# One region of rows moved to a multiple of 128 bytes, and two linear maps of the vector part joined into one, in a four-layer graph network

## The reference

```python
s_in = jnp.concatenate([agg[..., 0], agg[..., 1]], axis=1)
v_in = jnp.concatenate([agg[..., 2:5], agg[..., 5:8]], axis=1)
os1 = s_in @ w_f2o1_s / math.sqrt(2 * F)
ov1 = jnp.einsum('nmc,mb->nbc', v_in, w_f2o1_v) / math.sqrt(2 * F)
os1 = ssp(os1)                                   # softplus(x) - log 2
os2 = os1 @ w_f2o2_s / math.sqrt(B)
ov2 = jnp.einsum('nbc,bd->ndc', ov1, w_f2o2_v) / math.sqrt(B)
return jnp.concatenate([os2, ov2.reshape(n, -1)], axis=-1)
```

## Time and profile before

| | us |
|---|---|
| median of 3 runs | 2288.8 (2287.68 to 2291.94) |
| profiled execution | 2287.86 |
| its span, first to last instruction | 2285.8 |

### The profile page before, as it was taken

One profiled execution on the slowest core, in us unless ns is written; L12 is line 12 of the kernel. 1 busy time (PEld: TensorE's weight loads), 2 busy tenths in 40 slices (PEclk: granted clock), 3 DMA queues, 4 the chain that ended last, 5 costly groups with the idle time before them and its releaser, 6 DMA issues.

```text
span 2285.8 us, 36469 instructions
## 1 busy us (share of the span) xinstructions
PE 2223.5 (97%) x12307; PEld 1892.1 (83%) x12307; DVE 1487.8 (65%) x4613; ACT 1023.7 (45%) x2044; POOL 943.0 (41%) x931
## 2 busy tenths in 40 slices
PE   7999999979999999999999999999999999999996
PEld 6878778858899888888999999988887777778785
DVE  7777777754766856665345665267776776667675
ACT  3982112222365632222225665334444665666454
POOL 2017637745223234366532222023545554552542
PEclk9999999989999999999999999999999999999998
DMA  6434575443477758786226665456667776666541
GB/s 210 139 137 135 143 200 189 156 139 101 145 237 240 259 170 275 266 270 221 86 78 210 234 236 211 134 187 228 208 211 235 249 257 225 211 231 210 167 124 65
DMA packets 192415, 435.82 MB, mean 191 GB/s; under 512 B 45607, under 2 KB 74542, under 8 KB 191694
## 3 DMA queue, kind: packets, MB, share of 16 engines
q1 hardware_dynamic: 126954, 249.08, 31.9%
q0 software_dynamic: 65296, 184.67, 25.9%
HBM read 242.68 MB, written 190.96 MB: 190 GB/s over the span
## 4 chain that ended last, share of the span: by engine, by line
PE 67%; DVE 5%; ACT 3%; issue 2%; DMA 1%; POOL 0%; DVEq 0%; ACTq 0%; SPq 0%; POOLq 0%
PE g_h_ps L2575 7%; PE g_h_ps L2592 7%; PE g_h_ps L2577 6%; PE g_h_ps L2576 6%; PE g_h_ps L2593 6%; PE g_h_ps L2594 6%; PE g_h_ps L2617 5%; PE g_h_ps L2619 5%; PE g_h_ps L2618 5%; PE g_t_ps L77 4%; PE g_h_ps L1748 2%; PE g_h_ps L1750 2%; PE g_h_ps L1749 2%; PE g_sum_ps L995 1%; PE g_sum_ps L996 1%
## 5 line engine op out<-in xcount | busy, mean ns | idle before, releaser
L2709 ACT ACTIVATE g_act_t<-g_t_ps,g_b_col 128x256 f32<-128x256 f32 (+1 forms) x488 | 201.9, 466 | 398.3 <-PE g_t_ps L77 398.0
L2592 PE MATMUL g_h_ps<-g_x_hi,held_w_hi 128*128 128x256 f32 x1216 | 352.1, 290 | 0.0
L2593 PE MATMUL g_h_ps<-g_x_lo,held_w_hi 128*128 128x256 f32 x1216 | 343.8, 283 | 0.0
L2594 PE MATMUL g_h_ps<-g_x_hi,held_w_lo 128*128 128x256 f32 x1216 | 343.8, 283 | 0.0
L607 DVE CUSTOM_DVE_ANT_0 g_prod<-g_h_sb,g_a_rows 128x256 f32<-128x256 f32 x632 | 224.1, 419 | 78.4 <-ACT g_h_sb L498 70.8
L2617 PE MATMUL g_h_ps<-fc_w_hi,g_x_hi 128*128 128x512 f32 x632 | 270.9, 429 | 3.0 <-DVE fc_z L2995 2.2
L2575 PE MATMUL g_h_ps<-held_w_hi,g_x_hi 128*128 128x512 f32 x656 | 263.5, 402 | 0.0
L2577 PE MATMUL g_h_ps<-held_w_hi,g_x_lo 128*128 128x512 f32 x656 | 256.7, 391 | 0.0
L2576 PE MATMUL g_h_ps<-held_w_lo,g_x_hi 128*128 128x512 f32 x656 | 256.5, 391 | 0.0
L429 PE MATMUL g_h_ps<-g_w_hi,g_x_hi 128*128 128x512 f32 x616 | 243.4, 395 | 8.9 <-DVE g_x_lo L593 7.3
L2619 PE MATMUL g_h_ps<-fc_w_hi,g_x_lo 128*128 128x512 f32 x632 | 249.9, 395 | 0.0
(11 more groups left out here) (400 smaller groups left out, 4864.1 us busy)
## 6 DMA issues: line engine op xcount, KB each, us to landing
h<-g_h_sb SPq DMA_DIRECT2D x120, 512.0 KB, 4.5
g_x_in<-in_dram SPq DMA_DIRECT2D x40, 512.0 KB, 3.9
h<-g_rows_own SPq DMA_DIRECT2D x40, 512.0 KB, 5.0
h_cols<-g_h_sb SPq DMA_DIRECT2D x38, 512.0 KB, 5.3
xb_rows<-in_dram SPq DMA_DIRECT2D x19, 1024.0 KB
xb<-xb_rows SPq DMA_DIRECT2D x19, 1024.0 KB, 4.4
g_x_in<-h_cols SPq DMA_DIRECT2D x38, 512.0 KB, 6.7
g_x_in<-h SPq DMA_DIRECT2D x21, 512.0 KB, 5.8
```

What stands on the lines that cost most here:

```text
L2592: pe.matmul(out, wh, xh, start=(k == 0), stop=False)
L2593: pe.matmul(out, wh, xl, start=False, stop=False)
L2594: last = pe.matmul(out, wl, xh, start=False, stop=(k == KC - 1))
```

## The change

It has two parts. The first is in the layout: `Space.align` is new, and `node_layers` calls it with 128 before it takes `rows_at`, which then is 169344 = 1323 x 128. Everything from there to the end of the space moves up by 64 bytes.

The second is in painn. As no nonlinearity stands between the two maps of the vector part, their weights are multiplied on chip once: `join_weights` makes the 64x128 product in PSUM, and DVE scales it into `ov`. `w_f2o1_v` is loaded turned (`o1v_t`, 128x64) for that. `out_one` keeps the scalar part alone; `copy_sums_t` writes the turned vector sums into one of four buffers `vecs_t`, of 64 partitions, and `out_two` multiplies these by `ov`. The buffers `hid` and the copy into them go.

```diff
+        sb.align(P)
         rows_at = sb.end
...
     def out_one(self, pe, t):
...
-            pe.wait_ge(self.w_scaled, 2)
+            pe.wait_ge(self.w_scaled, 3)
...
-        pe.matmul(h.o1_ps[:, 0:P], h.o1s[:, :], h.sums_t[:, 0, :], start=True, stop=True)
-        pe.matmul(h.o1_ps[:, P:4 * P], h.o1v[:, :], h.sums_t[0:2 * f, 1:4, :], start=True, stop=True).then_inc(self.o1_done, 1)
+        pe.matmul(h.o1_ps[:, 0:P], h.o1s[:, :], h.sums_t[:, :], start=True, stop=True).then_inc(self.o1_done, 1)
+
+    def join_weights(self, pe):
+
+        h, f = self.hold, self.F
+        pe.wait_ge(self.w_in, 16 * 8)
+        pe.matmul(h.o1_ps[0:2 * f, 0:P], h.o1v_t[:, :], h.o2v[:, :], start=True, stop=True).then_inc(self.o1_done, 1)
...
         for c in range(3):
-            pe.matmul(h.o2_ps[:, (1 + c) * b:(2 + c) * b], h.hid[t % 4][:, c, :], h.o2v[:, :], start=True, stop=True)
+            pe.matmul(h.o2_ps[:, (1 + c) * b:(2 + c) * b], h.vecs_t[t % 4][:, c, :], h.ov[:, :], start=True, stop=True)
...
     def copy_sums_t(self, act, t):
...
+        if t >= 4:
+
+            act.wait_ge(self.o2_done, t - 3)
...
     def copy_hidden(self, act, t):
...
-            act.wait_ge(self.o2_done, t - 3)
             act.wait_ge(self.scal_done, t // 2 - 1)
-        act.activation(h.hid_s[t // 2 % 2][:, t % 2, :], h.o1_ps[:, 0:P], ACT.Copy)
-        act.activation(h.hid[t % 4][:, :, :].rearrange("p c e -> p (c e)"), h.o1_ps[:, P:4 * P], ACT.Copy).then_inc(self.o1_out, 1)
+        act.activation(h.hid_s[t // 2 % 2][:, t % 2, :], h.o1_ps[:, 0:P], ACT.Copy).then_inc(self.o1_out, 1)
...
-        dve.tensor_scalar(h.o1v[:, :], h.o1v_raw[:, :], (2 * f) ** -0.5, None, ALU.mult).then_inc(self.w_scaled, 1)
+        dve.wait_ge(self.o1_done, self.JOINED)
+        dve.tensor_scalar(h.ov[:, :], h.o1_ps[0:2 * f, 0:P], (2 * f) ** -0.5, None, ALU.mult).then_inc(self.w_scaled, 1)
...
+                    if g == PAINN_W + 3 * KC:
+                        pe.wait_ge(signals.finished, e2.past(ET, ET))
+                        painn.join_weights(pe)
+                    if g == CONV:
+                        pe.wait_ge(painn.w_scaled, 3)
```

More of the change, by code:

```diff
@@ L72, in __call__, with align @@
         return tensor
+    def align(self, unit):
+        self.end = -(-self.end // unit) * unit
 def turn_whole(pe, out, rows, ident):
@@ L1338 @@
     AHEAD = 4
+    JOINED = 1
     B = P
@@ L1389, in load_weights @@
             sp.dma_start(h.o1s_raw[(1 + c) * f:(2 + c) * f, :], self.w_o1s[f:2 * f, :]).then_inc(self.w_in, 16)
-        sp.dma_start(h.o1v_raw[:, :], self.w_o1v).then_inc(self.w_in, 16)
+        sp.dma_start(h.o1v_t[:, :], self.w_o1v).then_inc(self.w_in, 16)
         sp.dma_start(h.o2s[:, :], self.w_o2s).then_inc(self.w_in, 16)
@@ L1481, in out_one @@
     def out_one(self, pe, t):
-        h, f = self.hold, self.F
+        h = self.hold
         if t == 0:
-            pe.wait_ge(self.w_scaled, 2)
+            pe.wait_ge(self.w_scaled, 3)
         pe.wait_ge(self.st_out, 2 * t + 2)
@@ L1488, in out_one @@
             pe.wait_ge(self.o1_out, t)
-        pe.matmul(h.o1_ps[:, 0:P], h.o1s[:, :], h.sums_t[:, 0, :], start=True, stop=True)
-        pe.matmul(h.o1_ps[:, P:4 * P], h.o1v[:, :], h.sums_t[0:2 * f, 1:4, :], start=True, stop=True).then_inc(self.o1_done, 1)
+        pe.matmul(h.o1_ps[:, 0:P], h.o1s[:, :], h.sums_t[:, :], start=True, stop=True).then_inc(self.o1_done, 1)
[3 more added lines that the diff above has]
+        pe.matmul(h.o1_ps[0:2 * f, 0:P], h.o1v_t[:, :], h.o2v[:, :], start=True, stop=True).then_inc(self.o1_done, 1)
     def out_two(self, pe, t):
-        h, b = self.hold, self.B
+        h, b, f = self.hold, self.B, self.F
         pe.wait_ge(self.o1_out, t + 1)
@@ L1539, in copy_sums_t @@
         if t:
-            act.wait_ge(self.o1_done, t)
-        act.activation(h.sums_t[:, 0, :], h.turn_ps[:, 0:P], ACT.Copy).then_inc(self.st_out, 1)
-        act.activation(h.sums_t[0:2 * f, 1:4, :].rearrange("p c e -> p (c e)"), h.turn_ps[0:2 * f, P:4 * P],
+            act.wait_ge(self.o1_done, self.JOINED + t)
+        if t >= 4:
+            act.wait_ge(self.o2_done, t - 3)
+        act.activation(h.sums_t[:, :], h.turn_ps[:, 0:P], ACT.Copy).then_inc(self.st_out, 1)
+        act.activation(h.vecs_t[t % 4][:, :, :].rearrange("p c e -> p (c e)"), h.turn_ps[0:2 * f, P:4 * P],
                        ACT.Copy).then_inc(self.st_out, 1)
@@ L1547, in copy_hidden @@
         h = self.hold
-        act.wait_ge(self.o1_done, t + 1)
+        act.wait_ge(self.o1_done, self.JOINED + t + 1)
         if t >= 4:
-            act.wait_ge(self.o2_done, t - 3)
             act.wait_ge(self.scal_done, t // 2 - 1)
-        act.activation(h.hid_s[t // 2 % 2][:, t % 2, :], h.o1_ps[:, 0:P], ACT.Copy)
-        act.activation(h.hid[t % 4][:, :, :].rearrange("p c e -> p (c e)"), h.o1_ps[:, P:4 * P], ACT.Copy).then_inc(self.o1_out, 1)
+        act.activation(h.hid_s[t // 2 % 2][:, t % 2, :], h.o1_ps[:, 0:P], ACT.Copy).then_inc(self.o1_out, 1)
     def softplus(self, act, i):
@@ L2097, in node_layers @@
         p.u = split_rows(big("u", [P, 4 * 8 * F]), 4, 8 * F)
-        p.hid = [big(f"hid{s}", [P, 3, P]) for s in range(4)]
-        p.x_t, p.sums_t = big("x_t", [P, 4, P]), big("sums_t", [P, 4, P])
+        p.vecs_t = [big(f"vecs_t{s}", [2 * F, 3, P]) for s in range(4)]
+        p.x_t, p.sums_t = big("x_t", [P, 4, P]), big("sums_t", [P, P])
         p.pmsg = big("msg", [P, 10 * F])
@@ L2111, in node_layers @@
         low = Space(nc, "painn", small_at)
-        p.o1s, p.o1v, p.o2s, p.o2v = (low(n, [rows, P]) for n, rows in (("o1s", P), ("o1v", 2 * F), ("o2s", P), ("o2v", P)))
-        p.o1s_raw, p.o1v_raw = low("o1s_raw", [P, P]), low("o1v_raw", [2 * F, P])
+        p.o1s, p.ov, p.o2s, p.o2v = (low(n, [rows, P]) for n, rows in (("o1s", P), ("ov", 2 * F), ("o2s", P), ("o2v", P)))
+        p.o1s_raw, p.o1v_t = low("o1s_raw", [P, P]), low("o1v_t", [P, 2 * F])
         p.w_in_sb = low("w_in", [P, 2, F])
@@ L3224 @@
            g(0, "Wfc"), g(0, "bfc"), g(1, "weight"), np.stack([g(2, "w_in2f_s"), g(2, "w_in2f_v")], 1),
-           g(2, "W1"), g(2, "b1")[:, None], pw2, g(2, "w_f2o1_s"), g(2, "w_f2o1_v"), g(2, "w_f2o2_s"),
+           g(2, "W1"), g(2, "b1")[:, None], pw2, g(2, "w_f2o1_s"), g(2, "w_f2o1_v").T, g(2, "w_f2o2_s"),
            g(2, "w_f2o2_v"), g(3, "W").T, g(3, "b")]
```

## The result

| | us |
|---|---|
| before, median of 4 runs | 2290.37 (2287.68 to 2292.65) |
| changed kernel, median of 4 runs | 2270.14 (2268.23 to 2273.96) |
| ratio | 0.9923, 95% interval 0.9909 to 0.9937 |

By the ratio the change saves 17.6 us (14.4 to 20.8). The two medians lie 20.2 us apart, at the upper end of that interval; the profiled executions, which the rest of this text takes apart, took 2287.86 and 2270.06 us, 17.8 apart. The forecast was 22.5: right in direction, and the time lies in the range of 2260 to 2275, but the gain is 5 us smaller than forecast. The rest of this text finds these 5 us.

What follows compares the result with a forecast made beforehand. PE bounds the kernel, except in the conv stretch, where it already waits. Alignment 9.8 + edge sums 0.5 + joined map 12.0 - join 0.3 + shorter waits 0.5 = 22.5 us saved: 2266 us, own range 2262 to 2270, wider range 2260 to 2275.

Steps and rivals of the forecast that it cites:

- What bounds the kernel: fc, conv and painn stretches: PE bounds, so time off PE is time off the end, except in conv, where PE waits.
- rival 2: Painn stretch: DVE or ACT becomes the bound, PE waits for half of what it saved; 16.5 us gained, 2272; chance 0.11.
- The joined map: Painn tiles: removing L1490 saves 0.98 us, 64-row ends in out_two cost 0.38; net 0.60 a tile, 12.0 for 20.
- Rival 3: Painn tiles: the 0.33 us at L1490's ends was its own, not following the 64 rows; 7.6 us more, 2258; chance 0.07.
- 1896 x 5.7 ns = 10.8 us: fc products: with streamed weights on a multiple of 128 bytes, each of 1896 matmuls saves 5.7 ns.
- "half" of the conv stretch: fc with conv: alignment worth 2.1 us over 372 matmuls, half counted because PE idles 6 us; 10.8 - 1.0 = 9.8.
- given 0.5 back: Painn: PE's 2.0 us of waits for ACT's copy of the sums shrink by 0.5 us (bounds nothing and 2.0).
- The join there: fc tile 23: one matmul of two passes, 0.22 us, with one wait; 0.3 us of cost counted for everything.
- The edge sums' 0.5 us: Edge sums of the two earlier layers: 80 matmuls streaming src_hi gain 6 ns each from alignment, 0.5 us.
- Rival 1: fc products: the address does not make 233 of 227 ns; 12.2 us are left, 2276; chance 0.07.
- Rival 5: Painn stretch: PE idles between tiles, granted clock falls to 1.2 GHz, kernel slower, up to 2410; chance 0.02.

Runs made afterwards that it cites:

- 128-row version: Changed kernel with painn's vector part on 128 rows: two whole transposes, out_two's vector part as two matmuls against a block-diagonal joined map; 2265.53 us, ratio 0.9904.
- last version: 128-row version with x 64 bytes further on only in macro tiles whose products stream x over the held weights; 2255.31 us, ratio 0.9857.
- rows 32k: Changed kernel with x and the region 32 bytes higher, row k of fc_hi and fc_lo 32k bytes past the place alike to x; 2281.05 us, one run.
- faster version: Changed kernel with painn's vector work on whole 128-row passes instead of 64-row ones; 2265.53 us, ratio 0.9904.

## Why the prediction was right, and where it was wrong

**What bounds the kernel** was read rightly for two of three stretches. In the fc stretch and, less what PE's waits for the sums grew by, in the painn stretch time taken off PE reached the end. That the total still lies in the range is partly luck: the forecast's own range ended at 2270, and what lies above it was put in for rival 2, not for an alignment of half the size.

**The joined map** came out as worked: 0.98 - 0.38 = 0.60 us a tile was forecast, 12.3 us / 20 = 0.61 measured on PE's lines, and both numbers of the chain (0.86 and 0.42) are the ones named beforehand. That the ends of the 64-row work move with it is shown by the passes beside it and by taking the 64-row work away. The Trainium skill's "TensorEngine Tiling (Array Packing)", section "Key Properties", said that a change of mode drains the array, and the trace agrees: the passes at the two ends stand at 202 to 213 ns where those in the middle stand at 112, and of the 0.46 us a tile by which the 128-row version's lines are shorter, 0.36 are these ends (the rest is the transpose that it saves). That a drain is what fills them no run shows. Rival 3 is out.

**The step that failed** is the alignment's "1896 x 5.7 ns = 10.8 us", less "half" of the conv stretch. Alone it measures 4.6 us (2.7 to 6.6) where 9.8 + 0.5 stood. Three things were off, by the changed kernel's trace:

- The conv stretch. I saw PE idle for 6 us there and took half of its 2.1 us. It gave nothing: from step 412 to step 468 the changed kernel is 4.2 to 4.6 us ahead throughout, so a chain through ACT and DVE sets the pace there, and PE waits for `conv_t_lo`. The run at another pace shows it: six fc steps to a conv step take these waits away. The other kernels, at five steps, show it too: where the clock held, the stretch took 175.6 us in each of them, whether the fc products stood at 233 ns (before, the joined map alone), at 232 (rows 16 bytes apart, the region at 256) or at 228 (the last version). That is 0.0 in place of +1.0. With the fall of the clock it is -1.1: the stretch took 176.7 to 177.2 us in each of the five kernels where the clock fell once in it, and 178.4 where it fell twice.
- The painn stretch. fc products stood at 230 ns in the mean there, not 228, and its 396 products gave 1.1 us in place of 2.3. PE's waits for the sums rose by 1.0 us, where I had given 0.5 back, and that took the 1.1 away again. This rise belongs to the joined map: these waits are 3.0 us with the joined map alone too, 2.2 with the alignment alone and 2.0 before. What holds the distance at 230 ns in this stretch wasn't tried.
- The size: from one fc product to the next 5.3 ns in the fc stretch rather than 5.7 (233.4 to 228.1 in the mean), and nothing where transposes stand between two of them, beside some 150 of the 1032: 4.9 us in place of 5.9. The join there costs 0.36 where 0.3 was counted.

The edge sums' 0.5 us didn't come: 392 and 394 ns, where 396 and 392 stood before. Both their operands lie in the region and moved together, so by what the runs showed nothing changed for them. Their distances were 230 to 233 ns before and after, alike though their operands stand; why they are not at 228 stays open.

**The cause of the alignment's gain** was right as "the address" and wrong as "where the streamed operand starts". It is how the loaded and the streamed operand stand to each other modulo 256 bytes. The comparison with mlp and conv agreed only because their loaded tiles happened to stand alike to their weights. Rival 1 is out, and with it, for these products, the rule of the Trainium skill's "TensorE: Matmul & The Clock Gate", section "Back-to-back issue gap" (N / 2.4 plus 2.5 ns, 216 for 512 columns). That section calls it the gap of an isolated matmul, which the prediction left out, and gives some 131 ns for 512 columns in a sustained stream of loads and matmuls. Neither is what stands here: the measurement decides, and the distance moved between 227 and 233 by placement alone.

**Rival 5's mechanism is real, in another place.** I put the fall of the clock into the painn stretch; it came once in the conv stretch, behind a wait that had grown from 1.1 to 2.1 us. Its price was 1.6 us on PE and 1.1 in the stretch, too little to turn the sign. That the faster products brought it about is not shown: the last version has the same products and a wait as long, and its clock held; in two kernels with fc products at 232 to 233 ns (x alone moved by 64 bytes; rows 32k) the clock fell in this stretch too, behind the wait for `fc_z`. Rival 2 (waits for what was saved in painn) took 1.0 us in the changed kernel and 1.9 more in the faster version.

## What to carry to other kernels

Time saved per instruction is time saved at the end only in stretches where that engine never waits: multiply by stretch, and where it waits at all, count nothing rather than half, plus the risk of a slower clock behind a longer wait. When two similar operations differ, compare all of their operands' places before naming one of them as the cause: here the same number fitted "on a grid" and "alike to the other operand", and only moving the other one told them apart. Matmuls with half the rows cost little by themselves but at both ends; padding to whole rows can be cheaper.

## What the hardware showed that was not expected

- In long unbroken streams (fc, held weights, mlp) a 128x512 fp32r product repeats every 227 to 228 ns when its loaded and streamed operands start alike modulo 256 bytes, and every 232 to 233 ns at 32, 64 or 128 bytes apart. The edge sums' products, alike as well, stand at 230 to 233. For 128x256 products it is the other way round: 120 ns alike, 116 to 117 at 32 or 64 apart.
- With rows at mixed places the second and third product of every step, the well-placed ones too, took 390 to 397 ns. That the neighbours slow them is the nearest reading, and was not tested by itself.
- Behind some waits of 1.5 to 2.6 us TensorE ran at 1.2 GHz for several microseconds (granted clock 0.57 to 0.66 in the stretches shown); behind others as long it did not, such as the 2.5 us for `fc_z` in the changed kernel and the 2.1 us for `conv_t_lo` in the last version (granted clock 1.00 in the 4 us behind it). What decides it stays open.
